# Softmax denominators of two head groups in two columns of one 128x256 tile, in a two-layer attention kernel

## What is computed

```python
logits = jnp.einsum('abhqc,abhkc->abhqk', q, k)      # q already scaled
logits = logits + nonbatched_bias[:, None]           # layer 1: + mask_bias
weights = jax.nn.softmax(logits, axis=-1)
wavg = jnp.einsum('abhqk,abhkc->abhqc', weights, v)
gate = jax.nn.sigmoid(jnp.einsum('abld,ed->able', in_data, Wg) + gating_bias)
out = jnp.einsum('able,oe->ablo', gate * wavg, Wo) + bo
x = x + out
```

## Time and profile before

| | us |
|---|---|
| median of 3 runs | 3549.77 (3549.25 to 3550.27) |
| profiled execution, its own time | 3549.54 |
| its span | 3547.7 |
| VectorE (DVE) busy | 3411.0 (96%) |
| TensorE (PE) busy | 3377.9 (95%) |
| GpSimd (POOL) busy | 3011.8 (85%) |
| ScalarE (ACT) busy | 2893.4 (82%) |

### The profile page before, as it was taken

One profiled execution on the slowest core, in us unless ns is written; L12 is line 12 of the kernel. 1 busy time (PEld: TensorE's weight loads), 2 busy tenths in 40 slices (PEclk: granted clock), 3 DMA queues, 4 the chain that ended last, 5 costly groups with the idle time before them and its releaser, 6 DMA issues.

```text
span 3547.7 us, 122523 instructions
## 1 busy us (share of the span) xinstructions
PE 3377.9 (95%) x36136; PEld 2675.3 (75%) x36136; DVE 3411.0 (96%) x11685; ACT 2893.4 (82%) x5393; POOL 3011.8 (85%) x2066
## 2 busy tenths in 40 slices
PE   0699999999999999999969999999999999999998
PEld 0577887777887778877747778777787777877775
DVE  7799999999999999999949999999999999999997
ACT  0488988888988889888847888888888888888885
POOL 3388889888898888998837888988889888898896
PEclk9999999999999999999979999999999999999998
DMA  9555555555555555555544665556655566555663
GB/s 381 154 117 125 125 119 120 119 124 125 122 118 119 122 125 124 118 119 120 120 116 105 126 127 123 120 121 125 127 123 120 120 125 127 124 120 121 125 127 83
DMA packets 463188, 454.10 MB, mean 128 GB/s; under 512 B 55424, under 2 KB 453888, under 8 KB 462608
## 3 DMA queue, kind: packets, MB, share of 16 engines
q1 hardware_dynamic: 255312, 252.91, 30.4%
q10 hardware_dynamic: 207808, 200.33, 27.3%
HBM read 182.39 MB, written 67.24 MB: 70 GB/s over the span
## 4 chain that ended last, share of the span: by engine, by line
PE 92%; DVE 2%; DMA 2%; issue 1%; SPq 1%; ACT 1%; POOL 1%; DVEq 0%; ACTq 0%; POOLq 0%
PE proj_a L810 19%; PE proj_b L810 19%; PE av_bank L837 13%; PE max_bank L821 12%; PE exp_bank L826 12%; PE proj_a L866 10%; PE den_bank L848 6%; PE proj_b L858 1%; DVE stats L633 1%; DMA k_stack<-k_lo 1%; DMA probs<-in_xT 1%; DVE probs L715 0%; DVE max_bank L703 0%; SPq L352 0%; SPq L288 0%
## 5 line engine op out<-in xcount | busy, mean ns | idle before, releaser
L703 DVE CUSTOM_DVE_ANT_0 max_bank<-max_bank,bias_q 128x256 f32<-128x256 f32 x4096 | 1621.2, 432 | 64.8 <-PE max_bank L821 53.1
L454 POOL TENSOR_TENSOR probs_sum<-probs 128x1024 f32<-128x1024 f32 x508 | 1206.3, 2375 | 358.4 <-ACT probs L481 167.4
L715 DVE TENSOR_TENSOR probs<-exp_bank,bias_k 128x512 f32<-128x512 f32 x2048 | 1378.8, 674 | 10.9 <-PE exp_bank L826 10.9
L821 PE MATMUL max_bank<-k_stack,q_stack 96*128 96x256 f16 (+1 forms) x4096 | 787.5, 273 | 12.7 <-DMA k_stack<-k_lo 9.8
L826 PE MATMUL exp_bank<-q_stack,k_stack 100*128 100x256 f16 x4096 | 784.5, 272 | 9.6 <-DVE probs L715 7.2
L478 ACT ACTIVATE probs<-probs,mask_bias 128x1024 f32<-128x1024 f32 x512 | 560.4, 1142 | 36.4 <-issue 29.6
L481 ACT ACTIVATE probs<-probs 128x1024 f32<-128x1024 f32 x512 | 512.7, 1049 | 40.9 <-issue 34.9
L703 DVE DVE_READ_ACCUMULATOR2_ANT row_max<- 128x1 f32 x4096 | 533.0, 130 | 0.0
L837 PE MATMUL av_bank<-probs,v_sb 128*32 128x256 f32 x8192 | 497.9, 383 | 1.1 <-ACT probs L478 0.6
L826 PEld LDWEIGHTS exp_bank<-q_stack,k_stack 100*128 100x128 f16 x4096 | 394.3, 97 | 73.8 <-DVE probs L715 13.7
L821 PEld LDWEIGHTS max_bank<-k_stack,q_stack 96*128 96x128 f16 (+1 forms) x4096 | 394.2, 98 | 65.0 <-DMA k_stack<-k_lo 10.7
(11 more groups left out here) (139 smaller groups left out, 7003.0 us busy)
## 6 DMA issues: line engine op xcount, KB each, us to landing
q_stack<-q_hi SPq DMA_DIRECT2D x512, 128.0 KB
k_stack<-k_hi SPq DMA_DIRECT2D x512, 128.0 KB
q_stack<-q_lo SPq DMA_DIRECT2D x256, 128.0 KB
k_stack<-k_lo SPq DMA_DIRECT2D x256, 128.0 KB
y<-in_xT ACTq DMA_DIRECT2D x128, 256.0 KB, 3.7
layer_out<-y ACTq DMA_DIRECT2D x128, 256.0 KB, 4.2
y<-layer_out ACTq DMA_DIRECT2D x128, 256.0 KB, 3.7
out<-y ACTq DMA_DIRECT2D x128, 256.0 KB, 3.8
```

The costliest lines, as they stand in the source:

```text
L454: pool.tensor_tensor(probs_sum[:, g], pr[:, :, 0, :], pr[:, :, 1, :], ALU.add).then_inc(sum_ready, 1)
L703: op = dve.tensor_tensor_reduce(out=max_bank[h % 2][:, t, :], in0=max_bank[h % 2][:, t, :], in1=bias_q[:, h, t, :], scale=1.0 / FINE, scal ...
L715: dve.tensor_tensor(probs[:, r.ring(2), h], exp_bank[h % 2][:, :, :], bias_k[:, h], ALU.add).then_inc(logits_ready, 1)
L821: op = pe.matmul(bank_[:, t, :], q[0:n, t * P:(t + 1) * P], k[0:n, :], start=True, stop=True)
```

## The change

Group 0 and group 1 now add onto the same 128x256 half of `den_bank`. The matrix of ones becomes `head_ones`, two matrices of 128x32 that are zero but for column g. So in the 32 partitions of head j, partition 0 holds the denominator of group 0's head, partition 1 that of group 1's, and the others zero. VectorE turns 256 columns, and the reciprocal reads columns 0 and 1 of each of 8 blocks. `den_psum` counts once a row instead of twice, so all its waits are for both groups. GpSimd fills `head_ones` at the start with three memsets instead of one.

```diff
-        ones = sb("ones", [P, HC], f32)
+        head_ones = sb("head_ones", [P, HG, HC], f32)
...
-        den_turned = sb("den_turned", [P, HG * TOK], f32)
+        den_turned = sb("den_turned", [P, TOK], f32)
...
-            sp.wait_ge(zeroed, 3)
+            sp.wait_ge(zeroed, 5)
...
-            pool.memset(ones[:, :], 1.0).then_inc(zeroed, 1)
+            pool.memset(head_ones[:, :, :], 0.0).then_inc(zeroed, 1)
+            pool.wait_ge(zeroed, 1)
+            for g in range(HG):
+                pool.memset(head_ones[:, g, g:g + 1], 1.0).then_inc(zeroed, 1)
+                pool.wait_ge(zeroed, g + 2)
             for m in range(2):
-                pool.wait_ge(zeroed, m + 1)
+                pool.wait_ge(zeroed, m + 3)
                 pool.memset(stack[m][MASK_ROW:P, :, :, :], 0.0).then_inc(zeroed, 1)
-            pool.wait_ge(zeroed, 3)
+            pool.wait_ge(zeroed, 5)
...
-                wait(pool, den_psum, r.plus(-1).count(2, g + 1), pool_passed)
+                wait(pool, den_psum, r.plus(-1).count(1, 1), pool_passed)
...
-                    wait(dve, den_psum, r.plus(-2).count(2, h // 4 + 1))
+                    wait(dve, den_psum, r.plus(-2).count(1, 1))
...
-                dve.wait_ge(den_psum, r.count(2, 2))
-                dve.transpose(den_turned[:, :], den_bank[:, :, :].rearrange("p g t -> p (g t)")).then_inc(den_left, 1)
+                dve.wait_ge(den_psum, r.count(1, 1))
+                dve.transpose(den_turned[:, :], den_bank[:, 0, :]).then_inc(den_left, 1)
...
-                dve.reciprocal(recip_part[:, :], den_turned[:, :].rearrange("p (b o) -> p b o", o=HC)[:, :, 0]
+                dve.reciprocal(recip_part[:, :].rearrange("p (g b) -> p g b", g=HG),
+                               den_turned[:, :].rearrange("p (b o) -> p o b", o=HC)[:, 0:HG, :]
                                ).then_inc(recip_part_ready, 1)
...
-            pe.wait_ge(zeroed, 3)
+            pe.wait_ge(zeroed, 5)
...
-                            op = pe.matmul(den_bank[HC * j:HC * (j + 1), g, :], ones[:, :], part[:, j, :],
-                                           start=(t == 0), stop=(t == len(parts) - 1))
-                    op.then_inc(den_psum, 1)
+                            op = pe.matmul(den_bank[HC * j:HC * (j + 1), 0, :], head_ones[:, g], part[:, j, :],
+                                           start=(g == 0 and t == 0), stop=(g == HG - 1 and t == len(parts) - 1))
+                op.then_inc(den_psum, 1)
```

## The result

| | median, us | ratio to before, 95% interval |
|---|---|---|
| before, 21 runs | 3549.78 | |
| after, 21 runs | 3544.70 | 0.9984 (0.9978 to 0.9991) |

The kernel became 5.1 us faster, 0.16%. That is inside the 0.2% that I called no change, but clear of noise and outside my range of 3546.3 to 3552.3. Its profiled execution has a span of 3542.4 us, against 3547.7.

A forecast was written before the change was run, and what follows sets the result against it. TensorE was taken to bound the kernel, issuing each 13.02 us slot without a wait. The profiled 3549.54 us less 0.2 (0.1 a layer, in the slot before the pipe is full) gave 3549.3 us, range 3546.3 to 3552.3.

The forecast's parts named there:

- The bound: Steady slots: TensorE issues all 13.02 us without a wait; VectorE follows, some 0.12 us too early in every slot.
- VectorE's price: Transpose L733, 256 times: 695 ns down to 430, saving 68 us of VectorE's busy time, which nobody waits for.
- The matmuls and GpSimd's start: den_bank's 16 instructions a row adding onto the same half, and three chained memsets at the start: both priced at 0.
- Rival 2: In den_bank, adding onto the same columns costs a drain, 0.09 us in each of 254 rows, giving 3572; chance 0.04.
- rival 1: VectorE is the bound after all: some 248 full slots each shorten by 0.265 us, 66 us, giving 3484; chance 0.05.
- rival 3: VectorE's transpose L733 isn't shorter, its time being set by something other than columns: the same 3549.5; chance 0.04.
- Nothing upstream moves: Steady slots: VectorE's gap before L703 grows from 0.12 to about 0.38 us, nothing else shifts, and the saving is worth nothing.
- The term that I couldn't fix: Layer 1's loop: every other slot 0.04 us longer with k_lo's transfer, 2.3 us; VectorE's timing might move it either way.

## Why the prediction was right or wrong, point by point

- **The bound: right.** TensorE sets 13.02 us a slot, before and after. VectorE's saving is worth nothing that can be measured: a ratio of 1.0000 (0.9990 to 1.0010) by itself in the kernel before, and the change without it is as fast as with it, 3545.09 us against 3544.45.
- **VectorE's price: right.** 427 ns against 430 forecast, busy time 3343.7 against 3343, and the wait in front of the row maxima grew by 0.24 to 0.27 us a slot, as said.
- **The matmuls and GpSimd's start: right.** den_bank takes 0.97 us onto one half as onto two. Rival 2 is out, and rival 1 and rival 3 as well.
- **"Nothing upstream moves", and a sum without a term for addresses: wrong, and here the prediction failed.** The instructions that I priced at nothing (den_bank's 16, the memsets, the waits) did cost nothing. But I priced only the instructions that the diff adds or moves and never asked what a larger tile does to the tiles behind it. The line `head_ones = sb("head_ones", [P, HG, HC], f32)` moves x_in, the stacks and y by 128 bytes, their transfers take 5% less time, and with it go the 5.1 us that I had at 0.2. The change proper (shared columns, half the transpose, other waits) is worth nothing that can be measured: at equal addresses it is 3544.45 against 3544.14 us (two chips; ratios to before 0.9982 and 0.9986), 3550.35 against a before of 3548.78, and 3538.66 against 3536.34, each pair with overlapping intervals.
- **The term that I couldn't fix: the place was right, the cause not.** I put the long slots of layer 1 at 2.3 us, saw that they come with k_lo's transfer, and thought that VectorE's timing might move them. They were worth 2.3 to 2.6 us in that loop, and it was addresses that moved them. Some 2.2 us more came in layer 1's other slots, for which the sum had no term; the gain was 5.1 us, and I had allowed 3.0 around 0.2.
- **Open:** which wait gave the 2.2 us in layer 1's filling and emptying slots. The start, the change of layer and layer 0 scatter by 2 to 3 us between executions, so a part of the gain there can't be told. That addresses are the cause is shown by two pairs of kernels that differ in an unused tile alone, and that it comes by the transfers is shown by k_lo's landing for the long slots. For the other slots it is argued from the queues' shares, with the engines' own times unchanged. That the cuts at 256 bytes are how it comes about is the skill's account and was not seen in a trace.

The best version tried is the kernel before with three unused stretches, 3536.3 us, 12.4 us faster than before on its chip; aligning the biases too gives the same. The change on top of it gives nothing (3538.7 us, intervals overlapping).

## What to carry to other kernels

Before a change to a tile's size is judged by its instructions, look at what is allocated behind it: where a tile that transfers read or write starts, modulo 256 bytes, is part of the change. After a surprise of some tenths of a per cent, compare the queues' shares for the same packets and bytes before looking for a wait; and to separate a change from its side effect on addresses, run the kernel before with an unused tile of the same size. Where TensorE issues a slot without a wait, work taken from the engine that follows it buys only idle time there, even if that engine shows the higher busy share.

## What the runs showed of the hardware

Moving the same 453 MB in the same 463,120 packets, the two queues took 57.7% of 16 engines' span with the front tiles at 224 bytes past a multiple of 256, 55.0% at 96, 54.4% at 128, and 47.2% at a multiple (the tiles behind them moved too). With the front tiles alone at a multiple it was 48.1%, with recip to y alone 57.1%. k_lo's transfer, 128 KB from one tile of the core to another, went from 4.1 us at 224 to 3.8 at 96 and 3.1 at a multiple. A 128x256 block transpose out of PSUM takes 427 ns, one of 128x512 takes 695. Adding a second group of 32-column matmuls onto the same 256 columns costs what writing other columns does: 0.97 us for 16 instructions either way.
